# A two-layer post-norm decoder on one core: input in three transfers, the lift between the two sines, and the first Fourier group staged by VectorE

## The reference, cut to what matters

```python
def _fourier_kernel(x, proj_mat):
    p = jnp.einsum('blhd,dm->blhm', x, proj_mat) / math.sqrt(D_HEAD)
    return jnp.concatenate([jnp.cos(p), jnp.sin(p)], axis=-1) / math.sqrt(D_KMAP)
q_prime = _fourier_kernel(q, proj_mat)
k_prime = _fourier_kernel(k, proj_mat)
kv = jnp.einsum('blhm,blhd->bhmd', k_prime, v)
out = jnp.einsum('blhm,bhmd->blhd', q_prime, kv)
```

## Time and profile before

| what | us |
|---|---|
| median of 3 runs (lowest, highest) | 1683.41 (1680.9, 1689.48) |
| the profiled execution, its own time | 1688.41 |
| its span in the trace | 1686.6 |
| PE busy, share of the span | 1455.5, 86% |
| DVE busy | 1106.4, 66% |
| ACT busy | 916.2, 54% |
| POOL busy | 310.8, 18% |

### The profile page before, as it was taken

The page is one execution under the profiler, slowest core; times in us unless marked ns, Lnnn a source line. Parts: engine busy times, 40 slices in busy tenths (PEclk is TensorE's granted clock), DMA queues, the critical chain, the costliest instruction groups (busy, mean ns, idle before and its releaser), DMA issues. The chain is left out here.

```text
span 1686.6 us, 31393 instructions
## 1 busy us (share of the span) xinstructions
PE 1455.5 (86%) x12291; PEld 894.3 (53%) x12306; DVE 1106.4 (66%) x2343; ACT 916.2 (54%) x1255; POOL 310.8 (18%) x285
## 2 busy tenths in 40 slices
PE   5999869999798687888888847999999999999972
PEld 3666637777565333433334324566666666666542
DVE  2666646665332598898988952445567667776778
ACT  1332224444454588988888854445565565665433
POOL 2334234443000211101110012111111211210001
PEclk9999979999799799999999986999999999999995
DMA  4000000000000100000000000322222222222220
GB/s 160 2 2 2 2 20 14 12 11 2 1 1 1 51 1 1 1 1 1 1 1 1 1 10 7 71 62 63 68 59 57 69 69 60 60 66 63 57 53 16
DMA packets 39825, 50.73 MB, mean 30 GB/s; under 512 B 9216, under 2 KB 21632, under 8 KB 39296
## 3 DMA queue, kind: packets, MB, share of 16 engines
q1 hardware_dynamic: 39392, 48.06, 11.1%
q10 hardware_dynamic: 288, 0.67, 0.1%
HBM read 13.04 MB, written 2.10 MB: 9 GB/s over the span
## 5 line engine op out<-in xcount | busy, mean ns | idle before, releaser
L1521 DVE TENSOR_TENSOR l_px<-psum,l_share 128x1024 f32<-128x1024 f32 x64 | 78.4, 1225 | 155.5 <-PE psum L1240 101.8
L1381 ACT ACTIVATE l_prob<-psum,l_bias 128x1024 f32<-128x1024 f32 x64 | 71.3, 1114 | 173.6 <-PE psum L1220 173.6
L1229 PE MATMUL psum<-l_XT,l_A 128*128 128x256 f32 x512 | 132.4, 404 | 8.7 <-ACT l_th L1389 6.1
L1215 PE MATMUL psum<-l_th,l_XT 128*128 128x512 f32 x256 | 125.5, 613 | 0.9 <-DVE stream L1528 0.5
L1275 PE MATMUL psum<-l_px,l_N 128*128 128x256 f32 x512 | 124.6, 387 | 1.0 <-ACT l_r L1421 1.0
L1240 PE MATMUL psum<-l_prob,l_X 128*128 128x512 f32 x256 | 123.1, 603 | 0.0
L1229 PEld LDWEIGHTS psum<-l_XT,l_A 128*128 128x128 f32 x512 | 96.9, 200 | 23.0 <-ACT l_th L1389 8.1
L1502 DVE TENSOR_REDUCE l_top<-psum 128x8 bf16<-128x1024 f32 x64 | 78.1, 1221 | 44.8 <-PE psum L1290 44.8
L1275 PEld LDWEIGHTS psum<-l_px,l_N 128*128 128x128 f32 x512 | 94.7, 193 | 18.4 <-issue 4.7
L791 PE MATMUL psum<-f_projX,f_kT 64*128 64x512 f32 x256 | 72.7, 646 | 35.2 <-DVE f_frac L1050 19.2
L793 PE MATMUL psum<-f_qT,f_projX 64*128 64x512 f32 x256 | 72.3, 640 | 32.6 <-DVE f_frac L1050 24.7
(11 more groups left out here) (281 smaller groups left out, 3262.4 us busy)
## 6 DMA issues: line engine op xcount, KB each, us to landing
l_share<-l_recip SPq DMA_DIRECT2D x512, 64.0 KB, 2.0
early_weights<-in_weights SPq DMA_DIRECT2D x1, 2405.0 KB, 15.6
c_cs<-in_ctx SPq DMA_DIRECT2D x16, 128.0 KB, 2.1
f_qf<-in_l_mats SPq DMA_DIRECT2D x1, 2048.0 KB, 7.4
l_craw<-in_ctx SPq DMA_DIRECT2D x16, 128.0 KB, 2.2
out<-l_normed SPq DMA_DIRECT2D x16, 128.0 KB, 2.0
late_weights<-in_weights SPq DMA_DIRECT2D x1, 1089.0 KB, 11.0
relbias<-in_relbias ACTq DMA_DIRECT2D x1, 512.0 KB, 4.6
```

Source lines behind the costliest of these rows:

```text
L1215: nc.tensor.matmul(ps[:, SC + n, :], XT[:, q % 3, k, :, :], th[:, q % 2, k, 8 * n:8 * n + 8, :], start=True, stop=False)
L1229: last = nc.tensor.matmul(ps[:, RO + j // 2, (j % 2) * 256:(j % 2 + 1) * 256], A[:, QB * k + j, :], XT[:, q % 3, :, 1, :], start=True, sto ...
L1381: nc.scalar.activation(prob[:, b % 4, :, :], ps[:, SC:SC + 2, :], ACT.Exp, bias=bias[:, b:b + 1]).then_inc(s["exped"], 1)
L1521: nc.vector.tensor_tensor(px[:, q % 2, :, k, :], ps[:, GA:GA + 2, :].rearrange("p a (h s) -> p (a h) s", s=S), share[:, (b // 2) % 2, b % ...
```

## The change

```diff
+FIRST_TILES, NEXT_TILES = 4, 8
 # attention_phase
     with nc.Block() as block:
+        if not cross:
+            @block.sync
+            def _(sp):
+                c["load_rest"](sp)
 # PE, columns_of(d)
                 if cross:
                     pe.wait_ge(s["staged"], d + 1)
+                elif 2 * d >= FIRST_TILES:
+                    pe.wait_ge(c["x_next"] if 2 * d < FIRST_TILES + NEXT_TILES else c["x_rest"], 16)
...
-            pe.wait_ge(s["v_ones"], 1)
             columns_of(0)
 # DVE, soften(n)
                     dve.wait_ge(s["scores"], n + 1)
+                    if n == 0:
+                        dve.wait_ge(c["relbias_in"], 16)
 # fourier_phase, PE
-            pe.wait_ge(s["consts"], 6)
             columns_of(0)
             keys_and_values(0)
             queries(0)
+            pe.wait_ge(s["consts"], 6)
             angles(0)
 # fourier_phase, ACT
-            act.wait_ge(s["consts"], 6)
...
                 nc.scalar.activation(sin, view(frac[:, N % RING, :]), ACT.Sin, scale=-TWO_PI if n in ON_SCALAR else TWO_PI)
+                if N + 2 < ALL and (n + 2) % UPG in ON_SCALAR:
+                    lift(N + 2)
                 act.wait_ge(s["wrapped"], N + 1)
                 nc.scalar.activation(cos, view(wrap[:, N % RING, :]), ACT.Sin, bias=half_pi[:, :], scale=-TWO_PI).then_inc(s["feats"], 1)
...
             columns_of(0)
+            act.wait_ge(s["consts"], 6)
             for N in range(ALL + 5):
                 g, n = divmod(N, UPG)
-                if N + 1 < ALL and (n + 1) % UPG in ON_SCALAR:
-                    lift(N + 1)
 # fourier_phase, DVE
+            for t in range(T):
+                last = nc.vector.tensor_scalar(xs[:, t, :], c["stream"][:, t, :], c["moments"][:, t, 0:1], c["rstd"][:, t:t + 1],
+                                               ALU.subtract, ALU.mult)
+            last.then_inc(s["staged"], 1)
             nc.vector.memset(half_pi[:, :], HALF_PI).then_inc(s["consts"], 1)
 # fourier_phase, POOL
+            pool.wait_ge(s["staged"], 1)
             nc.gpsimd.tensor_tensor(projX[:, :, :], ...
             for g in range(G):
-                for t in range(T):
-                    ... staging of every group
+                if g >= 1:
+                    ... the same, of groups 1 to 7 only
 # build: issued on SP inside self-attention
+        def load_rest(sp):
+            x = ins["x"].rearrange("(n k) s d -> (k s) n d", k=2)
+            sp.dma_start(c["stream"][:, 12:NT, :], x[:, 12:NT, :]).then_inc(c["x_rest"], 16)
+            sp.dma_start(early[:, n_first:n_early], ins["weights"][:, n_first:n_early]).then_inc(loaded_rest, 16)
+            sp.dma_start(late[:, :], ins["weights"][:, n_early:n_w]).then_inc(loaded_rest, 16)
 # load block, SP
+                sp.dma_start(c["stream"][:, 0:4, :], x[:, 0:4, :]).then_inc(loaded, 16)
                 sp.dma_start(early[:, 0:n_first], ins["weights"][:, 0:n_first]).then_inc(loaded, 16)
-                sp.dma_start(c["stream"][:, :, :], ins["x"]...).then_inc(loaded, 16)
-                (the two transfers of the other weights)
+                sp.dma_start(c["stream"][:, 4:12, :], x[:, 4:12, :]).then_inc(c["x_next"], 16)
 # load block, ACT
                 act.dma_start(const[:, :], ins["const"]).then_inc(loaded, 16)
-                act.dma_start(c["relbias"][:, :, :], ins["relbias"]).then_inc(loaded, 16)
-                act.wait_ge(loaded, 64)
+                act.dma_start(c["relbias"][:, :, :], ins["relbias"]).then_inc(c["relbias_in"], 16)
+                act.wait_ge(loaded, 48)
```

More of the change, by code:

```diff
@@ L1091, in _ @@
                     pool.wait_ge(s["based"], g)
-                for t in range(T):
[L1093 to L1096, removed]
+                if g >= 1:
+                    for t in range(T):
+                        tile = g * T + t
+                        last = nc.gpsimd.tensor_scalar(xs[:, t, :], c["stream"][:, tile, :], c["moments"][:, tile, 0:1],
+                                                       c["rstd"][:, tile:tile + 1], ALU.subtract, ALU.mult)
+                    last.then_inc(s["staged"], 1)
                 pool.wait_ge(s["staged"], g + 1)
@@ L1795, in build @@
         }
+        def load_rest(sp):
+            x = ins["x"].rearrange("(n k) s d -> (k s) n d", k=2)
+            sp.dma_start(c["stream"][:, FIRST_TILES + NEXT_TILES:NT, :], x[:, FIRST_TILES + NEXT_TILES:NT, :]).then_inc(c["x_rest"], 16)
+            sp.dma_start(early[:, n_first:n_early], ins["weights"][:, n_first:n_early]).then_inc(loaded_rest, 16)
+            sp.dma_start(late[:, :], ins["weights"][:, n_early:n_w]).then_inc(loaded_rest, 16)
+        c["load_rest"] = load_rest
         loaded, loaded_rest = ctx.enter_context(nc.semaphore("loaded")), ctx.enter_context(nc.semaphore("loaded_rest"))
+        for n in ("x_next", "x_rest", "relbias_in"):
+            c[n] = ctx.enter_context(nc.semaphore(n))
         early_room = ExitStack()
@@ L1802, in _ @@
             def _(sp):
+                x = ins["x"].rearrange("(n k) s d -> (k s) n d", k=2)
+                sp.dma_start(c["stream"][:, 0:FIRST_TILES, :], x[:, 0:FIRST_TILES, :]).then_inc(loaded, 16)
                 sp.dma_start(early[:, 0:n_first], ins["weights"][:, 0:n_first]).then_inc(loaded, 16)
-                sp.dma_start(c["stream"][:, :, :], ins["x"].rearrange("(n k) s d -> (k s) n d", k=2)).then_inc(loaded, 16)
-                sp.dma_start(early[:, n_first:n_early], ins["weights"][:, n_first:n_early]).then_inc(loaded_rest, 16)
-                sp.dma_start(late[:, :], ins["weights"][:, n_early:n_w]).then_inc(loaded_rest, 16)
+                sp.dma_start(c["stream"][:, FIRST_TILES:FIRST_TILES + NEXT_TILES, :],
+                             x[:, FIRST_TILES:FIRST_TILES + NEXT_TILES, :]).then_inc(c["x_next"], 16)
             @block.scalar
```

## The result

Nine runs of the changed kernel have a median of 1678.25 us (1676.15 to 1680.36), nine of the kernel before 1685.74 us (1680.9 to 1689.48): a ratio of 0.9959, 95% interval 0.9945 to 0.9973, 7.5 us faster where 16.8 were forecast. The profiled executions differ by 8.0 us, 1688.41 against 1680.36. Up to the first keys of the Fourier phase the three starts had given 16.1 us, where 16.0 were forecast. From there to the end of that phase the changed kernel lost 5.9 us, where the prediction had 0.8 us of gain.

What follows compares the result with a forecast made beforehand. PE, busy 86% of the span, was taken as the bound, with gains in its idle time: 6.6 + 2.1 + 1.6 + 5.7 + 0.8 = 16.8 us off 1683.4 gives 1666.6 us; 8 in 10: 1656 to 1677.

Steps and rivals of the forecast that it cites:

- the three starts: Starts of the kernel, cross-attention and Fourier phase: PE's first transposes come earlier and the gain stays; 16.0 us.
- Load and `v_ones`: Kernel start: ACT waits for less input, 6.6 us; PE no longer waits for DVE's filling, 2.1 us.
- The 30 added waits: Added waits on PE: counted at nothing, since its sequencer runs ahead; 0.06 us each, 1.8 in all, in the range.
- Cross-attention: Start of cross-attention: without the wait on DVE's filling, the context's transposes move earlier by 1.6 us (1.3 to 2.0).
- Fourier start: Start of the Fourier phase: DVE stages four tiles, so PE transposes earlier; 5.7 us (4 to 5.8).
- The lift itself: Fourier groups: ACT's lift ahead of the cosine gains 0.1 us a group, 0.8 over seven; bounds -6 to +5.
- R4: The clock: slow PE stretches in every second group or so may change; none saves 6 us, one per group costs 6.
- R1: Fourier phase: the lifts pay in full, most of DVE's 25.9 us of waits go; 1647 us, chance 0.10.
- R3: Fourier phase: slower than before, lifts delay cosines and so PE; 49 us if all 48 do, 1716 us, chance 0.05.
- The bad bound of the clock: Fourier groups: a slow stretch in every one costs 6 us; priced only with the lift's bad bound, 1672 to 1677, chance 0.07.

Runs made afterwards that it cites:

- e2: Kernel before with only ACT's lift moved between the two sines; ratio 1.0006 to the kernel before.
- e1: Changed kernel with ACT's lift put back to the head of the iteration, the new starts kept; ratio 0.9911 to the kernel before, 15.0 us faster.
- e6: Changed kernel, unedited, run once more; ratio 0.9932 to the kernel before.
- e3: Changed kernel with only the lifts of units 10, 12 and 14 between the sines, the others at the head; ratio 0.9962 to the kernel before.
- e7: Changed kernel plus unread matmuls on PE (2 behind the angles of iterations 13 and 15, 1 in iteration 5); 1665.76 us, ratio 0.9877 to before.
- e8: Changed kernel with the lift at the head, plus unread matmuls (2 in iterations 13 and 15, 1 in 5); 1664.39 us, ratio 0.9865 to before.
- e9: Changed kernel with only lifts 10, 12 and 14 between the sines, plus light unread matmuls in iterations 5, 13 and 15; ratio 0.9882 to before.

## Why the prediction was wrong

- *Load and `v_ones`*: 8.7 forecast, 7.96 measured at PE's first transpose. The load gave 5.45 instead of 6.6 (ACT at 6.75): the weights landed at 6.7, near the bound by pace (7.0) and not at the 5.6 I took. PE, without the filling to wait for, began 0.70 behind ACT's start instead of 1.1. Self-attention gained 0.9: at the reciprocal behind it the kernel is 8.85 ahead (213.94, 205.09). Part of it may be that PE's durations became short earlier, counted from its first transpose (the second double's last projection took 0.77 us at 22.15, before 1.06 at 30.16); this is argued, not shown. The 30 added waits, at nothing in the sum and 1.8 us in the range, have no price in any run, but they can't have cost much where the phase gained.
- *Cross-attention*: 1.6 forecast, 1.58 measured (433.59 - 423.16 = 10.43, less 8.85). *Fourier start*: 5.7 forecast; from reciprocal to keys 12.10 became 6.32, 5.78. No run shows anything that would bring it down to 4, the lower end of this part's range: the projection again took 3.61 us beside the filling. The Trainium skill ("SBUF — State Buffer", SBUF: two separate sides) names, for the port pair that DVE and GpSimd share, DVE instructions in a two-port mode or with two inputs from the buffer. A filling has no input, so the 3.61 us are not at odds with that condition.
- *The lift itself*: 0.1 a group forecast, 0.16 measured in clean groups, and at the places named: lift 5 waits 3.05 us behind `combine`, DVE waits for keys 0.82 (1.07 forecast). DVE's waits for lifts did not fall from 25.9 to about 15: they are 26.2 in the phase, and 1.77 instead of 2.70 in a clean group. A wait that I had not seen is that of unit 4's products for `keep_kv` (0.65 us); the clean group is no longer for it, but it splits a gap.
- **The step that failed is R4**: "This widens the range, it does not move its middle." I took the falls of the clock as equally likely either way and put them at nothing in the sum, because I had worked the new order through for its times only. The runs showed nine low stretches instead of three: 3.3 us over six groups between the keys, 3.0 in the last group, against a gain of 0.4 in the first. That is the 5.9 us. By the four traces 3.2 to 3.5 of them come with the lift's new place and 2.4 to 2.7 with the new starts. R4's price was right in kind (a fall makes a group 1.64 us longer, so three more of them in the six groups would cost 4.9), but it had one fall in a group at most, and the 55.1 us groups have two, at 3.0 us together.
- *The rivals*: R1 is wrong, for the clean group is 0.16 shorter and not 0.8. R3's sign, a group more than 0.6 longer, nearly came, for the mean of six groups went from 52.94 to 53.49; but its mechanism, the lift's own delay, is not what lengthened them, since the groups without a fall are shorter. The bad bound of the clock came without that of the lift, and the prediction had priced only both together (0.07).
- *The base*: 1666.6 was reckoned off 1683.4, the median of three runs; nine gave 1685.7. That is 2.3 of the 11.6 us between forecast and result. By the two traces the other 9.3 are the Fourier phase (6.7: 5.9 lost instead of 0.8 gained), the last phase (1.6, put down to nothing) and about 1 in the difference between profiled executions and medians. The result lies 1.25 us outside the range of 8 in 10, so with the right base it would have lain inside: that the number was missed hung on the base as well, that the mechanism was missed did not.

What stays open is how much the moved lift costs on average, and why a gap is followed by a fall in one group and not in the next. The traces say 3.2 to 3.5 us for the lift; e2's ratio allows anything from 2 us faster to 4 slower. Whether the new starts cost their 2.4 us because the work begins 16 us earlier, or because the first group runs differently, no run separates.

## What to carry to other kernels

Where PE is busy for most of a loop and waits in short gaps, don't take the clock as fixed: here moving one ACT instruction, and even new starts before an unchanged loop, came with more falls of TensorE's clock, and these cost several times the 0.16 us a group that the move was worth. If the groups of a steady loop are not equally long, look at the granted clock first; a few matmuls without use, cut to fit the gaps, made them equal here and took off 8 to 14 us, while the same cut too long added 1.0 us to every group. Phase starts were the safer gain: what the first operation of a phase no longer waits for was still there at the start of each next one, though e1's Fourier phase, with its three more falls, was then 2.4 us longer.

## What the runs showed of the hardware

- The granted clock fell from 2.4 to 1.2 GHz for 3 to 4 us behind gaps of 1.8 to 2.5 us in PE's work, in some groups and not in others with the same gaps. In two profiled executions of one program the same groups were hit (e6 and the first profile). The same order of work begun 16 us earlier (e1) had the falls of before and three more. Over the 12 runs of e3 the mean clock varied from 0.936 to 0.953, so the number of falls is not always the same.
- With matmuls of no use in these gaps (1.98 us in that of 2.1 us) the granted clock stayed at 2.4 GHz through every middle group in the traces of e7, e8 and e9, and the groups of each were equal to 0.02 us.
- 385 KB behind 256 KB of x in 512-byte rows landed 5.5 us after their issue, 3.8 us when they went first.
- GpSimd's projection (128x2048) took 3.61 us with a filling of 1.76 us on DVE inside it, in both kernels.
